# Gated two-layer cross-attention block: context loads of layer 1 issued on ACT's DMA queue, inverse row sums ahead of the low pass on DVE

## What is computed

```python
# X: layer-normalised x, encoder_out: the raw context
Q  = (X @ Wq.T + bq).reshape(b, 56, 16, 64)
KV = (encoder_out @ Wkv.T + bkv).reshape(b, 1500, 16, 128)
K, V = KV[..., :64], KV[..., 64:]
scores  = einsum('bqhd,bkhd->bhqk', Q, K) / 8
weights = softmax(scores, axis=-1)
attn = einsum('bhqk,bkhd->bqhd', weights, V).reshape(b, 56, 1024)
x = x + tanh(g_xattn[1]) * (attn @ Wo.T + bo)
```

## Time and profile before

| | us |
|---|---|
| median of 3 runs | 1336.8 (1331.76 to 1341.48) |
| the profiled execution, its own time | 1342.3 |
| its span | 1340.6 |
| PE busy | 1157.7 (86%) |
| DVE busy | 896.5 (67%) |
| ACT busy | 697.8 (52%) |
| POOL busy | 509.4 (38%) |
| mean granted TensorE clock | 0.951 of full speed |

### The profile page before, as it was taken

The page is one execution under the profiler, slowest core; times in us unless marked ns, Lnnn a source line. Parts: engine busy times, 40 slices in busy tenths (PEclk is TensorE's granted clock), DMA queues, the critical chain, the costliest instruction groups (busy, mean ns, idle before and its releaser), DMA issues.

```text
span 1340.6 us, 27799 instructions
## 1 busy us (share of the span) xinstructions
PE 1157.7 (86%) x10054; PEld 658.5 (49%) x10056; DVE 896.5 (67%) x1250; ACT 697.8 (52%) x967; POOL 509.4 (38%) x344
## 2 busy tenths in 40 slices
PE   0769899999999997887978898989989899998974
PEld 0325556566665656434434454545545454554542
DVE  6456666666666663677777666767767676776667
ACT  0435455555555545455665555565555556555642
POOL 6147766666656613323032222232222223222320
PEclk9979899999999998799998898999989899898996
DMA  5144334544443343030067798898778888787540
GB/s 157 51 123 140 106 116 136 139 124 123 135 137 119 110 107 83 0 47 1 1 101 136 135 147 140 141 152 132 140 137 148 142 135 148 136 142 140 107 76 14
DMA packets 262934, 150.99 MB, mean 113 GB/s; under 512 B 233392, under 2 KB 244128, under 8 KB 262880
## 3 DMA queue, kind: packets, MB, share of 16 engines
q1 hardware_dynamic: 256624, 147.11, 53.6%
q10 hardware_dynamic: 6256, 3.16, 1.0%
HBM read 61.93 MB, written 12.80 MB: 56 GB/s over the span
## 4 chain that ended last, share of the span: by engine, by line
PE 57%; DMA 14%; DVE 13%; issue 8%; ACT 5%; ACTq 3%; DVEq 0%; POOL 0%; another core or an unknown queue 0%; SPq 0%; POOLq 0%
PE bank L863 11%; PE bank L845 10%; PE bank L720 7%; DMA region<-u_w 7%; DMA region<-wg_sb 7%; PE bank L744 5%; PE bank L748 5%; PE bank L813 4%; PE bank L761 4%; ACTq L385 3%; DVE neg_max L1538 2%; DVE region L1688 2%; DVE e_row L1499 2%; PE bank L885 2%; ACT region L1193 2%
## 5 line engine op out<-in xcount | busy, mean ns | idle before, releaser
L1499 DVE CUSTOM_DVE_ANT_0 e_row<-bank,region 112x1500 f32<-112x1500 f32 x128 | 220.1, 1719 | 126.4 <-PE bank L720 125.0
L1193 ACT ACTIVATE region<-bank 125x896 f32<-125x896 f32 x192 | 176.0, 917 | 203.5 <-PE bank L748 203.5
L1538 DVE TENSOR_REDUCE neg_max<-bank 128x1 f32<-128x1500 f32 x112 | 192.3, 1717 | 112.9 <-PE bank L845 112.9
L845 PE MATMUL bank<-region 128*128 128x500 f16 x1008 | 234.4, 378 | 3.2 <-ACT e_row L1220 1.8
L1229 ACT COPY region<-bank 128x768 f16<-128x768 f16 x224 | 177.9, 794 | 109.0 <-PE bank L813 109.0
L1220 ACT ACTIVATE e_row<-bank,neg_shift 128x1500 f32<-128x1500 f32 x112 | 169.2, 1511 | 66.5 <-DVE neg_shift L1542 65.8
L546 POOL CAST wg_sb<-e_row 128x1500 f16<-128x1500 f32 x56 | 81.8, 1461 | 244.6 <-ACT e_row L1220 133.4
L546 POOL CAST u_w<-e_row 128x1500 f16<-128x1500 f32 x56 | 80.6, 1439 | 237.8 <-ACT e_row L1220 227.6
L845 PEld LDWEIGHTS bank<-region 128*128 (+1 forms) x1008 | 97.3, 98 | 107.0 <-ACT e_row L1220 2.3
L744 PE MATMUL bank<-row_of,region 112*128 112x448 bf16 x384 | 137.8, 359 | 7.9 <-ACT region L1193 7.9
L863 PE MATMUL bank<-region,g_w 125*128 125x384 f16 (+1 forms) x576 | 140.0, 380 | 0.0
(11 more groups left out here) (218 smaller groups left out, 1532.8 us busy)
## 6 DMA issues: line engine op xcount, KB each, us to landing
region<-region SPq DMA_DIRECT2D x192, 96.0 KB, 2.2
region<-split_rows SPq DMA_DIRECT2D x24, 750.0 KB
c_in<-in_ctx SPq DMA_DIRECT2D x16, 750.0 KB
split_rows<-region SPq DMA_DIRECT2D x16, 750.0 KB
region<-in_mask_Bx1xSxS_if SPq DMA_DIRECT2D x32, 328.1 KB
g_w<-split_rows SPq DMA_DIRECT2D x8, 750.0 KB
x_norm_t<-inverse_rows SPq DMA_DIRECT2D x16, 256.0 KB, 4.8
x_norm_t<-inverse_rows SPq DMA_DIRECT2D x16, 192.0 KB, 3.6
```

The costliest lines, as they stand in the source:

```text
L845: last = pe.matmul(score_banks1(par, t)[:, k, :], q1[:, ql, b, 128 * t:128 * (t + 1)], c_t1[par][:, 4 * k:4 * k + 4, cl, 0:KP], start=(ql ...
L1193: act.activation(p0[:, 2 * i:2 * i + 2, :], ring0("s", h, i)[0:KP, :, 0:HALF_ROWS], ACT.Exp, scale=SCALE0)\
L1499: dve.tensor_tensor_reduce(out=masked.rearrange("p (a k) -> p a k", a=3), in0=bank[0:R0, 0:3, 0:4 * KP], in1=mask_bias[par][:].rearrange(" ...
L1538: dve.tensor_reduce(neg_max[:, t:t + 1], score_banks1(par, t), AX.XY, ALU.max, negate=True)\
```

## The change

Both loads move from SP's queue to ACT's. SP no longer issues them. ACT issues the first at the end of its step 3, the second at the end of its step 5 (on SP it stood in step 4). They wait for the same counts as before. On DVE the reciprocal of the row sums of tile t goes ahead of the low half of tile t. Nothing is added to or taken from what is computed.

```diff
@@ SP, layer1
-                    if t == 3 and not (isinstance(b, int) and b + 2 >= B):
-                        sync_split_in(sp, b + 2)
-                    if t == GROUPS1[1][0] and not last:
-                        sync_keep(sp, b + 1, 1 - par)
@@ new functions
+        def act_split_in1(act, b):
+
+            act.wait_ge(sem("c_turned1"), 16 * b)
+            act.dma_start(c_split1[0:KP], split_rows[b]).then_inc(sem("split_in1"), 16)
+
+        def act_keep1(act, b, par):
+
+            wait(act, sem("pv_done1"), 4 * (b - 1))
+            act.dma_start(c_keep1[par], split_rows[b]).then_inc(sem(f"kept1_{par}"), 16)
@@ ACT, layer1
                         act_high1(act, *turn, 0)
                     if has_turn:
                         act_high1(act, *turn, 1)
+                    if t == 3 and not (isinstance(b, int) and b + 2 >= B):
+                        act_split_in1(act, b + 2)
+                    if t == 5 and not last:
+                        act_keep1(act, b + 1, 1 - par)
@@ DVE, layer1
                     if not (last and t == T1 - 1):
                         dve_max1(dve, *nxt)
+                    dve_inv1(dve, b, par, t)
                     dve_low1(dve, b, par, t)
-                    dve_inv1(dve, b, par, t)
```

## The result

The change makes the kernel slightly slower: 1346.95 us median (1342.17 to 1350.86, 6 runs) against 1336.17 us of the kernel before (1329.66 to 1341.48, 6 runs). The ratio is 1.0085 with a 95% interval of 1.0049 to 1.0121. The prediction was 1276 us, with a range of 1262 to 1345 and a chance of 0.70 for faster. It was wrong, and the time fell beyond the range.

What follows compares the result with a forecast made beforehand. PE was taken as bound by stands behind transposes that loads on five engines delay. Profiled 1342.3 us, less 64.3 for idle and low clock, plus 3 for ACT's issues, gave 1281.0; less 5.5 to the median, about 1276, range 1262 to 1345.

Steps and rivals of the forecast that it cites:

- What bounds the kernel before: Layer 1's batches: loads on five engines hold tile transposes; PE's idle of 43.5 us and low clock of 20.8 total 64.3.
- I take 1 us: Assumed delay of a tile transpose meeting a load on ACT's queue, between bounds of 0 and 6.25 us; taken as hidden.
- The 368 packets of the earlier trace: Small transpose packets passed before a stop, 33 on each of 11 engines; read as turns of about 32 packets.
- R2: Rival: the first load on ACT's queue catches tile 3's transpose; PE waits 50.4 us before the second product; chance 0.33.
- ACT finishes its copy at 1043.87 and would issue the load there: First load's issue on ACT: 0.57 us before 1044.44, its packets from 1045.2, after tile 3's begin at 1044.6.
- The slack of tile 3: Tile 3's transpose would land at 1047.1 undelayed; PE needs it at 1049.23, leaving 1.1 us after 1 us delay.
- R2a: Rival: tile 3's transpose held, PE idle 50.4 us before the second product, clock stays; 1326 us, chance 0.15.
- R2b: Rival: the same idle before the second product, and PE's clock falls each time, 36.4 us more; 1362 us, chance 0.18.
- ACT's issues: 29 load issues on ACT, 0.27 to 0.49 us each; 0.1 us each sticks out, 3 us, at worst 110 us.
- The bound of 19.18 us: An early ACT issue was held 19.18 us; cited for load issues being held when engines are full.
- The reciprocal first: On DVE, costs nothing; releases PE 5 us earlier during low-half waits, brings nothing where the queue move removes the wait.
- R1: Rival: moving loads to ACT's queue brings nothing, only DVE's earlier reciprocal acts, saving 32 us; 1308 us, chance 0.13.

Runs made afterwards that it cites:

- e6: Kernel before with split_rows of 128 rows instead of 125, both loads on SP's queue, reciprocal behind the low half: 1265.61 us.
- e8: Kernel before with the reciprocal first and split_rows of 128 rows instead of 125, both loads on SP's queue: 1266.99 us.
- e11: Kernel before with the reciprocal first and each layer 1 load of 125 rows cut into DMAs of 112 and 13 rows, on SP's queue: 1269.39 us.
- e10: The change, but ACT waits for its own last copy to complete before issuing the first load: 1362.69 us.
- e7: The change with split_rows of 128 rows instead of 125, both loads on ACT's queue: 1268.20 us.
- e1: The change without its reciprocal edit: both loads on ACT's queue, reciprocal behind the low half: 1345.94 us.
- e2: Kernel before with only the reciprocal moved first, both loads still on SP's queue: 1329.05 us.
- e3: The change with the second load put back on SP's queue, only the first on ACT's: 1346.41 us.
- e4: The change with the first load put back on SP's queue, only the second on ACT's: 1319.78 us.
- e5: The change, but ACT issues the first load one step later, at the end of step 4: 1403.04 us.

## Why the prediction was wrong

*What bounds the kernel before* was read rightly. The stands come from the two loads, each holding the transposes because it occupies five engines, and they cost somewhat more than was said: with them gone (e6 to e8, e11) the time is 1266 to 1269 us, where the forecast for their going was 1276. The profiled span of e6 is 1340.6 - 1263.6 = 77.0 us shorter, where the prediction had 64.3: 52.0 us less outside PE's busy time (it had 43.5) and 25.0 us less of busy time with the same work (it had 20.8 for the clock).

*"I take 1 us"* is the step that failed. It is the delay of a transpose that meets a load on the other queue, chosen between 0 and 6.25 us. The 368 packets of the earlier trace rows were read as blocks of about 32 packets that an engine takes in one turn. Measured are turns of one packet (6.5 beside 6.0 an engine in the change, 40 beside 38 packets in e10); the 33 packets an engine are how far the eleven free engines run ahead before they stop. The upper bound was nearly the right value: tile 3 lands after 9.2 us instead of 3.8, 5.4 us late. Less the 2.1 us of slack that is 3.3 us, and PE stands 3.16. The earlier trace rows had shown one for one already, and the prediction named them as evidence for R2; they should have outweighed an inference from a stop.

*"ACT finishes its copy at 1043.87 and would issue the load there"* failed too, and would have mattered less: ACT's issue runs ahead of its copies, by 1.2 us before the copy begins. The load goes out ahead of tile 3's transpose instead of behind it. With the timing that was assumed (e10) the loss is larger, not smaller.

*The slack of tile 3* (2.1 us to PE's second product) was right, and PE's stand is where R2 put it. R2's 50.4 us of PE idle stand against 48.1. Its R2a (1326) and R2b (1362) lie on either side of 1347. In between is the clock: R2b had 36.4 us for it and R2a none. The change's PE is busy for 1162.9 - 1134.7 = 28.2 us longer than that of e7, which does the same work without the stands. In e10, which has R2's order of issue, R2b's number comes out, 1362 against 1362.7, but in part by luck: PE stands 60.9 us there and not 50.4, and nine tenths of the transpose had passed ahead of the load and not three tenths. The mechanism had been worked out and priced; it was given 0.33 where it should have led.

*ACT's issues* cost nothing visible: 0.27 us each in the median, 0.54 at most (L1238, L1243). The bound of 19.18 us did not come into play.

*The reciprocal first* brings nothing in the change (e1 against the change) and nothing without stands (e6 against e8), as predicted. By itself it brings 7 us, not the 28 that R1 worked out, because the stand moves and stays nearly as long, and the low clock moves with it (e2).

*R1's rule*, for which the prediction named the Trainium skill ("DMA: Bandwidth & Descriptors", rules for kernel authors), says that spreading DMAs over queues only saves issue time. It holds here for the rate of a load (60 packets in 3 us on SP's queue, 42 in 2 us on ACT's) and not for this kernel's time: the queue of the first load costs 1.3% (e3 against e2), that of the second brings 0.7% (e4 against e2), because the queue decides which transfers a load meets. For the time it holds where the loads are spread over 16 engines (e7 against e8).

## What to carry to other kernels

Count on how many DMA engines a transfer runs before asking on which queue it goes: a load of 125 partitions on 5 engines held up every transpose beside it, and three rows of padding or a split into 112 + 13 were worth 5%, more than any reordering. A queue that is served in order also protects what is ahead in it (tile 3 lands after 3.8 us where the load stands behind it on SP's queue, after 9.2 where it does not). So before moving a large load to another queue, look which transfer it will now overtake, and how soon that one is wanted. A stand that disappears at one place is worth its length only if the next thing wanted is not late too.

## What the hardware showed beyond that

- Where two hardware queues advanced on the same engines they did so packet by packet, whatever the size: 256 bytes against 6144 (6.5 to 6.0 packets an engine, 40 to 38 packets in e10) as well as 1024 against 6144 (112 to 114). But in the change the load first ran alone, 42 packets in 2 us to none.
- A DMA transpose moves its packets on all 16 engines nearly in step: with five engines occupied the other eleven got 33 packets ahead and stopped.
- ACT's queue issues a DMA ahead of ACT instructions before it in the program that have not begun: 1.2 us before the copy in front of it. A wait for that copy's semaphore is what holds it back (e10).
- A small transfer waits on the queue with the transposes: one of 2 KB held ACT up to 14.0 us (e5).
- PE's clock after a stand: the stand of 4.73 us in the kernel before was followed by a granted clock of 0.50, and the one of 3.16 us in the change by a stretch of 4 us with 0.62; the one of 1.48 us was not. In e6 to e8, which have no stands of this kind in layer 1's batches, the mean granted clock over the span is 0.97, in the kernel before 0.951.
